# Layer-norm statistics of two tiles by one VectorE instruction, with reordered logits, stores and waits, in a fused attention and expert kernel

## The chip, the cores and the metric

The kernel runs on one core of a Trainium2 chip. The metric is the device time of one execution in microseconds; the time of the kernel before is the median of three runs. The engines are PE (TensorE), VectorE (DVE), ScalarE (ACT), GpSimd (POOL) and the DMA queues, the first of which SyncE (SP) issues.

## What is computed

The reference, cut to what matters. `x` has 32 sequences of 256 tokens of 128 numbers; there are 8 experts with a hidden width of 512.

```python
h = _layernorm(x) * (1 + ca) + sa
x = x + ga * _L0_attn_ref(h, ...)
h = _layernorm(x) * (1 + cb) + sb
x = x + gb * _L0_ffn_ref(h, ...)

# attention, per sequence, cumulative sums along the tokens
K = exp(linear(x, Wk1, bk1)); K_cum = cumsum(K) + 1e-06
S = cumsum(K * V) / K_cum;    Q = sigmoid(linear(x, Wq1, bq1))
O_ar = S * Q
E = V[1:] - O_ar[:-1]
K2 = sigmoid(0.02 * linear(shifted x, Wk2, bk2) / sqrt(D))
S2 = cumsum(K2 * E);          O_ma = S2 * Q2
out = linear(O_ar + O_ma, Wproj, bproj)

# experts: each token goes to the expert of its largest logit
assign = argmax(x @ centroids.T)
xn = (x - mean(x)) * rsqrt(var(x) + 1e-05) * ln_g[e] + ln_b[e]
y = x + relu(xn @ W1[e] + b1[e]) @ W2[e] + b2[e]
```

So there are three layer norms: of x, of the sum after the attention (called z here), and of the rows of each expert tile.

## The kernel before

**Chunk stage.** The 64 tiles of 128 tokens are worked on in 16 chunks of four tiles (two sequences). A loop over c, written out for each engine by hand, runs several chunks at once: x statistics are made for chunk c + 5 on VectorE (`x_stats`, `x_means`), normalised on GpSimd (`normalise_x`, L493) for chunk c + 3, transposed on PE (L793) and scaled on ScalarE (`turned_x`, L947) for chunk c + 2; keys, k2 and q products follow (L735, L742, L745), VectorE makes the cumulative sums (`k_sum` L1188, `kv_sum` L1200, `error_sum` L1234, which makes S2), and PE adds up x, the shift, Oar and Mp products in one bank (L757, L759, L766, L783). ScalarE copies the sum to the row buffer (`sum_of`, L912). For chunk c - 1 VectorE makes the z statistics (`z_stats`, `z_means`), GpSimd normalises z two steps behind (L501), PE transposes it (`turn_z`, L691), ScalarE scales it (`turned_z`, L920), and for chunk c - 3 PE makes the logits (L714) and turns the result back (`turn_back`, L691 on h2T), which ScalarE writes to the rows (`rows_of`, L926). Every second step VectorE routes eight tiles (`route`, `place`) and PE makes rank products (`ranks`, L680 and L685). GpSimd scatters rows of 385 numbers to the expert regions in DRAM (`scatter`, L538) and multiplies the projection weights with the gates in c = 0 to 5 (`gate_weights`, L509).

**Statistics.** A `bn_stats` of 128 numbers writes six values: count, mean and count times variance of the even elements, then of the odd ones. `bn_aggr` joins them to mean and variance in `mv`. ScalarE turns the mean to its negative (`minus_means`, L933) and makes exp(-0.5 ln(var + eps)) (L1014, L1025); the first four chunks get their negative mean on VectorE and their power on GpSimd (`first_rstd`).

**Plan.** After chunk 9 VectorE makes a first plan of expert tiles (`plan_first`), some of it in step c = 14. ScalarE reads expert numbers of the plan with `expert_of` (L296).

**Expert stage.** 36 tiles: 25 of 256 rows of one expert, then 11 of two blocks of 128 rows. For tile j: load (SP, L442 or L447), statistics (`tile_stats`, L1462, `tile_means`, L1469) three tiles ahead, normalisation (L1475), transposes (L830), ScalarE's `norm_of_expert` (L1064), first layer (L817, or L821 for blocks), relu (L1044, L1051, for blocks the last part on VectorE, L1484), second layer (L845), VectorE's bias, residual and gate (L1501, L1674, L1692, L1709), and GpSimd's indirect stores of tile j - 2 (`store`, L613). `take_ids` (L605) makes the row numbers of a store from the loaded rows, three tiles ahead.

**What sets the order.** Every engine has its own queue and works it off in the order written. A wait for a semaphore at the head of a queue holds up all that is behind it. Nothing is scheduled by a program. `keep_going(n)` is n transposes of an identity into an unused bank.

## Time and profile before

| | us |
|---|---|
| median of three runs | 334.05 |
| lowest and highest | 332.75, 334.86 |
| the profiled execution | 336.69 |
| its span, first to last instruction | 335.0 |

| engine | busy us | share of the span | instructions |
|---|---|---|---|
| PE matmuls | 297.9 | 89% | 1889 |
| VectorE | 268.0 | 80% | 926 |
| ScalarE | 248.6 | 74% | 556 |
| GpSimd | 237.4 | 71% | 370 |

The mean granted clock of PE is 0.964: the profile shows stretches at 1.2 GHz instead of 2.4 GHz between 10 and 50 us, one near 165 us, and the end. The chunk stage takes the first 168 us or so, a stage in which both overlap follows to about 194 us, and the expert stage runs to 320 us. The rest is the last stores. Busy time of an engine says little by itself: where an engine waits, what it waited for must be read from the chain of waits (what released what) and the timeline (instructions in order of time).

### The profile page before, as it was taken

To read this page: it belongs to the slowest core of one execution; us is meant where nothing else is said; L and a number is where in the kernel's file an instruction comes from. 1 tells how busy PE (TensorE), PEld (TensorE's weight loads), DVE (VectorE), ACT (ScalarE), POOL (GpSimd) and SP (SyncE) were. 2 spreads that over 40 slices of the span, in tenths; PEclk is the share of its full clock that TensorE was granted. 3 is DMA by queue.
4 is the path that set the end of the run, shared out by engine and by line. 5 is a ranking of instruction groups with operands and counts; after the bars stand their busy time and mean duration, and the time that the engine had idled before them with its cause. 6 is when DMAs were issued, how large, how long until landed. Compare 5 with 4: busy or idle time off the path is not lost.

```text
span 335.0 us, 8136 instructions
## 1 busy us (share of the span) xinstructions
PE 297.9 (89%) x1889; PEld 237.1 (71%) x1889; DVE 268.0 (80%) x926; ACT 248.6 (74%) x556; POOL 237.4 (71%) x370
## 2 busy tenths in 40 slices
PE   8797998898989989899898999999999999888930
PEld 7474555564656656465587899999999999888930
DVE  5798999999999999989886387898666665758850
ACT  2759788989899999999768666776677776766510
POOL 7984334787989888978646878778888855544770
PEclk9979779999999999999799999999999999999985
DMA  7343288424438786634396789877888777778300
GB/s 213 80 117 94 80 241 217 127 63 155 157 116 233 208 233 200 168 103 149 104 291 206 229 269 302 284 238 228 229 226 234 208 238 226 220 232 233 102 18 0
DMA packets 49429, 60.87 MB, mean 182 GB/s; under 512 B 5557, under 2 KB 38095, under 8 KB 49379
## 3 DMA queue, kind: packets, MB, share of 16 engines
q1 hardware_dynamic: 42806, 43.11, 47.0%
q0 software_dynamic: 6368, 16.82, 13.7%
q8 instruction: 17, 0.28, 0.3%
q10 hardware_dynamic: 208, 0.41, 0.3%
q14 instruction: 30, 0.25, 0.3%
HBM read 39.90 MB, written 20.87 MB: 181 GB/s over the span
## 4 chain that ended last, share of the span: by engine, by line
PE 53%; DVE 13%; issue 13%; ACT 11%; POOL 3%; SPq 2%; DMA 1%; POOLq 0%; ACTq 0%; DVEq 0%
PE bank L845 15%; PE bank L817 13%; PE bank L639 3%; PE bank L821 3%; PE bank L742 2%; POOL out_dram L613 2%; PE bank L745 2%; PE bank L783 2%; DVE shared L1234 2%; PE bank L735 2%; PE bank L691 2%; PE bank L830 2%; PE bank L766 2%; ACT shared L947 2%; PE bank L714 1%
## 5 line engine op out<-in xcount | busy, mean ns | idle before, releaser
L613 POOL DMA_INDIRECT out_dram<-shared,ids x71 | 72.1, 1015 | 34.2 <-DVE shared L1709 15.9
L538 POOL DMA_INDIRECT expert_rows<-rows,slots x64 | 65.5, 1023 | 15.8 <-issue 15.4
L845 PE MATMUL bank<-w_all,shared 128*128 x568 | 69.4, 275 | 0.4 <-issue 0.3
L845 PEld LDWEIGHTS bank<-w_all,shared 128*128 128x128 f32 x568 | 66.2, 192 | 0.9 <-issue 0.9
L1044 ACT ACTIVATE shared<-bank,par 128x256 f32<-128x256 f32 x100 | 40.9, 472 | 15.3 <-PE bank L817 15.3
L501 POOL TENSOR_SCALAR zz<-rows,negm,rstd 128x128 f32<-128x128 f32 x64 | 33.4, 532 | 24.8 <-ACT rstd L1025 17.3
L817 PE MATMUL bank<-shared,early 128*128 128x256 f32 x200 | 47.8, 382 | 0.3 <-ACT shared L1044 0.3
L817 PEld LDWEIGHTS bank<-shared,early 128*128 128x128 f32 x200 | 36.1, 190 | 4.5 <-issue 0.3
L493 POOL TENSOR_SCALAR xh<-x_in,negm,rstd 128x128 f32<-128x128 f32 x64 | 28.6, 458 | 9.0 <-DVE shared L1207 8.6
L1501 DVE TENSOR_TENSOR shared<-bank,b_bc 128x256 f32<-128x256 f32 (+1 forms) x42 | 14.7, 366 | 23.6 <-PE bank L845 22.9
L1064 ACT ACTIVATE shared<-bank,par 128x256 f32<-128x256 f32 (+1 forms) x46 | 22.7, 515 | 6.4 <-PE bank L830 4.0
L821 PE MATMUL bank<-shared,rows 128*128 128x128 f32 x168 | 21.9, 278 | 2.9 <-DVE shared L1484 2.9
L1051 ACT ACTIVATE shared<-bank,par 128x128 f32<-128x128 f32 x64 | 18.8, 370 | 7.2 <-PE bank L821 7.1
L783 PEld LDWEIGHTS bank<-wg,Mp 128*128 128x128 f32 x128 | 17.5, 199 | 7.7 <-issue 7.7
L821 PEld LDWEIGHTS bank<-shared,rows 128*128 128x128 f32 x168 | 20.1, 192 | 3.9 <-DVE shared L1484 3.9
L959 ACT ACT_TABLE_LOAD x16 | 20.5, 1283 | 0.3
L954 ACT ACT_TABLE_LOAD x16 | 20.5, 1283 | 0.3
L979 ACT ACTIVATE blnv<-bmv,epsv 128x2 f32<-128x2 f32 (+1 forms) x36 | 10.5, 293 | 13.4 <-issue 7.1
L766 PE MATMUL bank<-wg,shared 128*128 128x128 f32 x128 | 19.9, 302 | 0.0
L757 PE MATMUL bank<-x_in,ident 128*128 128x512 f32 x32 | 17.0, 614 | 3.2 <-ACT rows L912 3.2
L1188 DVE TENSOR_TENSOR_SCAN shared<-seq_mask,bank 128x512 f32<-128x512 f32 x16 | 19.4, 1212 | 0.5 <-ACT bank L964 0.5
L920 ACT ACTIVATE h2T<-bank,mod 128x256 f32<-128x256 f32 x32 | 16.3, 559 | 4.3 <-PE bank L691 4.3
(216 smaller groups left out, 699.6 us busy)
## 6 DMA issues: line engine op xcount, KB each, us to landing
early<-in_L_ffn_W_dram SPq DMA_DIRECT2D x25, 256.0 KB
x_in<-expert_rows SPq DMA_DIRECT2D x15, 385.0 KB, 4.2
rows<-in_L_ffn_W_dram SPq DMA_DIRECT2D x21, 256.0 KB
x_in<-in_L_attn_x_dram SPq DMA_DIRECT2D x16, 256.0 KB, 3.2
rows<-gates_rows SPq DMA_DIRECT2D x32, 128.0 KB, 5.2
full<-expert_rows SPq DMA_DIRECT2D x10, 385.0 KB
expert_rows<-pad_rows SPq DMA_DIRECT2D x9, 385.0 KB, 8.4
full<-expert_rows SPq DMA_DIRECT2D x11, 192.5 KB
```

The source lines that it names most:

```text
L493: pool.tensor_scalar(xh[:, a % 2, t, :], x_in[:, a % XR, t, :], negm[:, a, 0, t:t + 1], rstd[:, a, 0, t:t + 1], ALU.add, ALU.mult).then_in ...
L501: pool.tensor_scalar(zz[:, y % 2, t, :], rows[:, y % RR, t, W:W + D], negm[:, y + 6, 1, t:t + 1], rstd[:, y + 6, 1, t:t + 1], ALU.add, ALU ...
L538: pool.indirect_dma_start(rows_dram, bass.IndirectOffsetOnAxis(ap=slots[:, c * CN + t:c * CN + t + 1], axis=0), rows[:, c % RR, t, :], Non ...
L613: pool.indirect_dma_start(out_rows, bass.IndirectOffsetOnAxis(ap=ids[:, u % IR, t:t + 1], axis=0), u_sb[:, k, t, :], None, bounds_check=T - 1,
L766: pe.matmul(ps_proj[:, t * P:(t + 1) * P], Oar[:, c % 2, s, l:l + P], wg[:, CS * c + s, :], start=False, stop=False)
L783: mm = pe.matmul(ps_proj[:, t * P:(t + 1) * P], Mp[:, c % 2, s, l:l + P], wg[:, CS * c + s, :], start=False, stop=(t == CN - 1))
L817: mm = pe.matmul(hidden_at(j, f), w1_of(j, 0)[:, f * P:(f + 1) * P], zT[:, j % 2, :], start=True, stop=True)
L821: mm = pe.matmul(hidden_at(j, f)[:, t * P:(t + 1) * P], w1_of(j, t)[:, f * P:(f + 1) * P], zT[:, j % 2, t * P:(t + 1) * P], start=True, st ...
L845: mm = pe.matmul(out_at(o, t), hid[:, k, f, t * P:(t + 1) * P], of_expert(w2_all, e, f * D, (f + 1) * D), start=(f == 0), stop=(f == FC - 1))
L954: act.activation(lnK[:, q % 2, :, :], Kc[:, :, :], ACT.Ln, scale=LN_SCALE, bias=epsk[:, :]).then_inc(s_ln, 1)
L1044: r = act.activation(hid[:, j % 2, f, :], hidden_at(j, f), ACT.Relu, bias=par[:, 2 + f, bass.ds(e, 1)])
L1064: z = act.activation(zT[:, n % 2, h], ps_t[:, h], ACT.Identity, bias=par[:, 1, bass.ds(e, 1)], scale=par[:, 0, bass.ds(e, 1)])
```

## The change

Statistics:

- One `bn_stats` reads two tiles with their elements alternating, so that its even elements are those of one tile and its odd elements those of the other. Its six values then are count, mean and 128 times the variance of each. `bn_aggr`, `xbn`, `zbn`, `mv` and `negm` are gone; the values stay in `bn`, whose room is kept for every step. ScalarE's logarithm takes a scale of 1/128.
- GpSimd subtracts the mean itself; the negations on ScalarE and VectorE are gone.
- In the expert stage a tile with a single block reads it twice. The statistics wait for what `bn_aggr` waited for.
- At c = 14 the z statistics stand behind `error_sum`.

Order and waits:

- PE makes the logits and turns them back ahead of the Oar products.
- PE runs eight more identity transposes at c = 14, ahead of the k2 and q products.
- `gate_weights` of c = 2 to 5 waits for the `error` of one step later.
- ScalarE reads the first two expert numbers at c = 15 ahead of `rows_of`, and `rstd_of(14)` stands ahead of `sum_of(15)`.
- GpSimd takes the ids of tile j behind the stores of iteration j, not those of tile j + 3 ahead of them.

The diff, cut to its core:

```diff
-        mv = sb("mv", [P, STEPS, 2, CN, 2])
+        bn = sb("bn", [P, STEPS, 2, CN, 3])
...
-                    pool.tensor_scalar(zz[:, y % 2, t, :], rows[:, y % RR, t, W:W + D], negm[:, y + 6, 1, t:t + 1],
-                                       rstd[:, y + 6, 1, t:t + 1], ALU.add, ALU.mult).then_inc(s_zz, 1)
+                    pool.tensor_scalar(zz[:, y % 2, t, :], rows[:, y % RR, t, W:W + D], bn[:, y + 6, 1, t, 1:2],
+                                       rstd[:, y + 6, 1, t:t + 1], ALU.subtract, ALU.mult).then_inc(s_zz, 1)
...
-                    pool.wait_ge(s_E, c + 1)
+                    pool.wait_ge(s_E, c + 1 if c < 2 else c + 2)
...
-            for j in range(-3, NJ + 2):
-                if in_b(j + 3):
-                    take_ids(j + 3)
+            for j in range(NJ + 2):
...
+                if in_b(j):
+
+                    take_ids(j)
...
+                if in_a(z):
+                    logits(z)
+                    turn_back(z)
+                if in_a(c):
                     pe.wait_ge(s_Oar, c + 1)
...
-                if in_a(z):
-                    logits(z)
-                    turn_back(z)
...
+                if c == NC - 2:
+
+                    keep_going(8, ps_t)
...
-                    act.activation(lnv[:, i, kinds, :], mv[:, i, kinds, :, 1], ACT.Ln, bias=epsv[:, :]
+                    act.activation(lnv[:, i, kinds, :], bn[:, i, kinds, :, 2], ACT.Ln, scale=1.0 / D, bias=epsv[:, :]
                                    ).then_inc(s_lnv, 1)
-                    minus_means(i, kinds)
...
+                if c == NC - 1:
+
+                    act.wait_ge(s_planned, 1)
+                    of_first = [expert_of(act, n) for n in range(2)]
                 if in_a(z):
                     rows_of(z)
...
             experts = [norm_of_expert(0)]
+            rstd_of(NC - 2)
             sum_of(NC - 1)
-            rstd_of(NC - 2)
             experts.append(norm_of_expert(1))
...
+            def stats_of_two(into, rows_of_two):
+
+                return dve.bn_stats(into.rearrange("p t k -> p (t k)"), rows_of_two.rearrange("p t d -> p d t"))
...
-                dve.bn_stats(zbn[:, t, :], rows[:, o % RR, t, W:W + D]).then_inc(s_bnz, 1)
...
+                stats_of_two(bn[:, o + 6, 1, 2 * h:2 * h + 2, :], rows[:, o % RR, 2 * h:2 * h + 2, W:W + D]
+                             ).then_inc(s_bnz, 1)
...
-                for t in parts(n):
-                    dve.bn_aggr(bmv[:, n % 4, t, :], bbn[:, n % 4, t, :]).then_inc(b_aggr, 1)
+                two = full(n)[:, :, 0:D] if len(parts(n)) == FS else full(n)[:, 0:1, 0:D].to_broadcast([P, FS, D])
+                stats_of_two(bbn[:, n % 4, :, :], two).then_inc(b_bn, 1)
...
-                if in_a(o):
+                if in_a(o) and not first:
                     z_stats(o, 0)
-                    z_stats(o, 1)
...
+                if first:
+                    z_stats(o, 0)
                 if in_a(o):
-                    z_stats(o, 2)
-                    z_stats(o, 3)
+                    z_stats(o, 1)
...
-                if in_a(a) and c >= 0:
+                if in_a(a):
                     x_stats(a, 0)
                     x_stats(a, 1)
-                if in_a(a) and c >= 0:
-                    x_stats(a, 2)
-                    x_stats(a, 3)
-                    for t in range(CN):
-                        x_means(a, t)
```

The first place is VectorE in a chunk step without routing, from the product with k2 to the ratio of the next step. `rows` holds z and `x_in` holds x. Before:

```order
L1228 SCALAR_TENSOR_TENSOR bank<-bank,shared 128x2x255
L1142 BN_STATS zbn<-rows 128x6 x2
L1234 SCALAR_TENSOR_TENSOR shared<-seq_mask,bank 128x512
L1142 BN_STATS zbn<-rows 128x6 x2
L1240 SCALAR_TENSOR_TENSOR Mp<-bank,shared 128x2x256
L1147 BN_AGGR mv<-zbn 128x2 x4
L1131 BN_STATS xbn<-x_in 128x6 x4
L1136 BN_AGGR mv<-xbn 128x2 x4
L1207 TENSOR_TENSOR shared<-shared 128x512
```

The same piece of VectorE's order in the changed kernel, where line numbers are some ten lower:

```order
L1221 SCALAR_TENSOR_TENSOR bank<-bank,shared 128x2x255
L1129 BN_STATS bn<-rows 128x6
L1227 SCALAR_TENSOR_TENSOR shared<-seq_mask,bank 128x512
L1129 BN_STATS bn<-rows 128x6
L1233 SCALAR_TENSOR_TENSOR Mp<-bank,shared 128x2x256
L1129 BN_STATS bn<-x_in 128x6 x2
L1200 TENSOR_TENSOR shared<-shared 128x512
```

Eight statistics instructions and eight aggregations of a step have become four statistics instructions; each stands where its pair stood.

The second place is PE at c = 14, from the z transposes to the Mp products; `centT` marks the logits, the transposes of h2T are `turn_back`, and the products of `wg` and `shared` are those with Oar. Before:

```order
L691 MATMUL bank<-ident,zz 128x128 x4
L757 MATMUL bank<-x_in,ident 128x512
L759 MATMUL bank<-shift_in,ones_bf 128x512
L766 MATMUL bank<-wg,shared 128x128 x4
L714 MATMUL bank<-centT,h2T 128x8 x4
L691 MATMUL bank<-ident,h2T 128x128 x4
L742 MATMUL bank<-shared,wT 128x512
L745 MATMUL bank<-shared,wT 128x512
L783 MATMUL bank<-wg,Mp 128x128 x4
```

The same piece of PE's order in the changed kernel:

```order
L688 MATMUL bank<-ident,zz 128x128 x4
L754 MATMUL bank<-x_in,ident 128x512
L756 MATMUL bank<-shift_in,ones_bf 128x512
L711 MATMUL bank<-centT,h2T 128x8 x4
L688 MATMUL bank<-ident,h2T 128x128 x4
L767 MATMUL bank<-wg,shared 128x128 x4
L636 MATMUL bank<-ident 128x128 x8
L739 MATMUL bank<-shared,wT 128x512
L742 MATMUL bank<-shared,wT 128x512
L784 MATMUL bank<-wg,Mp 128x128 x4
```

The Oar products have moved behind the logits and their way back, as in every step from c = 3 on, and eight identity transposes stand ahead of k2.

The third place is ScalarE between the stages, from the scaling of chunk 12 to the rows of chunk 13; L296 reads the plan. Before:

```order
L920 ACTIVATE h2T<-bank,mod 128x256 x2
L926 ACTIVATE rows<-bank 128x4x128
L979 ACTIVATE blnv<-bmv,epsv 128x2
L982 ACTIVATE brstd<-blnv 128x2
L920 ACTIVATE h2T<-bank,mod 128x256 x2
L979 ACTIVATE blnv<-bmv,epsv 128x2
L982 ACTIVATE brstd<-blnv 128x2
L296 TENSOR_LOAD plan
L296 ISA x2
L1064 ISA
L1064 ACTIVATE shared<-bank,par 128x256
L912 ACTIVATE rows<-bank 128x4x128
```

The same piece of ScalarE's order in the changed kernel:

```order
L921 ACTIVATE h2T<-bank,mod 128x256 x2
L293 TENSOR_LOAD plan
L293 ISA x2
L293 TENSOR_LOAD plan
L293 ISA x2
L927 ACTIVATE rows<-bank 128x4x128
L973 ACTIVATE blnv<-bbn,epsv 128x2
L977 ACTIVATE brstd<-blnv 128x2
L921 ACTIVATE h2T<-bank,mod 128x256 x2
L973 ACTIVATE blnv<-bbn,epsv 128x2
L977 ACTIVATE brstd<-blnv 128x2
L1065 ISA
```

Both reads of the plan have moved ahead of `rows_of(12)`, from the place just ahead of the first two `norm_of_expert`.

## Rows read from the trace of the kernel before

**Rows 1.** Windows by stage: from:to, length, busy PE, PEld, DVE, ACT, POOL, clock, DMA share, GB/s

```profile
52.00:149.00 97.00, 89.45 (x502) 58.32 (x503) 94.58 (x263) 91.03 (x162) 79.15 (x127) 1.00 0.58 166
...
194.20:277.50 83.30, 83.21 (x591) 77.29 (x590) 61.54 (x262) 58.51 (x157) 65.85 (x82) 1.00 0.82 243
```

**Rows 2.** Timeline of VectorE at c = 6: start us, length us, engine, line, what

```profile
84.55 0.47 DVE L1142 BATCH_NORM_STATS2 zbn<-rows 128x6 f32<-128x128 f32 x2
84.94 1.19 DVE L1234 TENSOR_TENSOR_SCAN shared<-seq_mask,bank 128x512 f32<-128x512 f32 x1
...
87.87 0.85 DVE L1131 BATCH_NORM_STATS2 xbn<-x_in 128x6 f32<-128x128 f32 x4
88.76 0.38 DVE L1136 BATCH_NORM_AGGREGATE mv<-xbn 128x2 f32<-128x6 f32 x4
89.05 0.77 DVE L1207 TENSOR_TENSOR shared<-shared 128x512 f32<-128x512 f32 x1
```

**Rows 3.** Chain of waits, 96 to 111 us: start us, length us, engine and line

```profile
99.31 0.45 PE bank L793 x4
...
100.95 0.63 PE bank L691 x4
...
106.02 0.86 PE bank L742 x2
...
108.70 0.44 PE bank L793 x4
```

**Rows 4.** Timeline of PE, z transposes of c = 3 and c = 13

```profile
51.98 0.63 PE L691 MATMUL bank<-ident,zz 128*128 128x128 f32 x4 [1.20 <-ACT shared L947]
...
148.95 0.63 PE L691 MATMUL bank<-ident,zz 128*128 128x128 f32 x4 [0.51 <-ACT shared L947]
```

**Rows 5.** Timeline of GpSimd, gate weights of c = 4 and three z normalisations

```profile
69.35 1.84 POOL L509 TENSOR_TENSOR wg<-wg,wT 128x256 f32<-128x256 f32 x2
...
77.65 2.17 POOL L501 TENSOR_SCALAR zz<-rows,negm,rstd 128x128 f32<-128x128 f32 x4 [1.46 <-ACT rstd L1025]
...
88.57 2.26 POOL L501 TENSOR_SCALAR zz<-rows,negm,rstd 128x128 f32<-128x128 f32 x4
...
97.72 2.29 POOL L501 TENSOR_SCALAR zz<-rows,negm,rstd 128x128 f32<-128x128 f32 x4
```

**Rows 6.** Groups by line and shape, VectorE: count, then busy us, mean ns, idle before

```profile
L1188 DVE TENSOR_TENSOR_SCAN shared<-seq_mask,bank 128x512 f32<-128x512 f32 x16 | 19.4, 1212 | 0.5 <-ACT bank L964 0.5
...
L1131 DVE BATCH_NORM_STATS2 xbn<-x_in 128x6 f32<-128x128 f32 x64 | 13.6, 274 | 0.6 <-DMA x_in<-in_L_attn_x_dram 0.6
...
L1194 DVE TENSOR_TENSOR bank<-bank,shared 128x512 f32<-128x512 f32 x16 | 11.0, 690 | 0.4 <-ACT shared L947 0.2
```

**Rows 7.** Line L1221: duration ns min/median/max; and its instruction of c = 5

```profile
L1221 DVE SCALAR_TENSOR_TENSOR shared<-shared x16: 678/682/1430, 19.7 to 168.8; 128x510 f32<-128x510 f32 x16
...
72.49 0.68 DVE L1221 SCALAR_TENSOR_TENSOR shared<-shared 128x510 f32<-128x510 f32 x1
```

**Rows 8.** Chain of waits, at the start

```profile
12.34 0.86 DVE xbn L1131 x4
```

**Rows 9.** Timeline of PE at c = 14, k2 and Mp products

```profile
163.24 1.31 PE L742 MATMUL bank<-shared,wT 128*128 128x512 f32 x2 [1.43 <-DVE shared L1234]
...
166.15 1.69 PE L783 MATMUL bank<-wg,Mp 128*128 128x128 f32 x8
```

**Rows 10.** Timeline of ScalarE between the stages, the first two `norm_of_expert`

```profile
176.24 0.56 ACT L1064 ACTIVATE shared<-bank,par 128x256 f32<-128x256 f32 x1 [0.86 <-PE bank L830]
...
178.31 0.56 ACT L1064 ACTIVATE shared<-bank,par 128x256 f32<-128x256 f32 x1 [0.50 <-issue]
```

**Rows 11.** Waits by engine and line, whole span: us in total, times, longest

```profile
PE bank L821 <- DVE shared L1484: 2.9, 4, 1.2
```

**Rows 12.** Timeline of GpSimd, first and last of the last seven stores

```profile
317.81 1.00 POOL L613 DMA_INDIRECT out_dram<-shared,ids  x1 [0.52 <-issue]
...
325.59 0.97 POOL L613 DMA_INDIRECT out_dram<-shared,ids  x1 [0.30 <-issue]
```

97 lines of the change are left out of this document (29 added, 68 removed).

## The prediction

> **What bounds the kernel now.** I read three views in this order: the windows by stage, the chain of waits, and the timeline of one engine at a time inside one chunk step.
>
> The windows [rows 1] give the stages. From 52 to 149 us VectorE is busy 94.6 of 97.0 us, while PE, ScalarE and GpSimd have 89.5, 91.0 and 79.2. From 194 to 277 us PE has 83.2 of 83.3 us and VectorE only 61.5: work taken from VectorE there is worth nothing. So the question is what the statistics cost inside a chunk step, and what the next limit is.
>
> The timeline of VectorE [rows 2] prices them by the distance between starts, since instructions overlap. Two statistics instructions of 128 elements take 84.94 - 84.55 = 0.39 us. Four x statistics and the wait for their last one take 88.76 - 87.87 = 0.89, the four aggregations and the wait for them 89.05 - 88.76 = 0.29. With two z pairs (0.78) and four z aggregations (0.28, nearly as for x) a step spends 2.24 us on statistics.
>
> The chain of waits [rows 3] shows the next limit. From the end of the x transposes at 99.31 + 0.45 = 99.76 to the z transposes at 100.95 PE waits 1.19 us for ScalarE (`turned_x`, L947). From there PE works without a pause to 108.70 + 0.44 = 109.14, that is 8.19 us. PE order and this one answer of ScalarE form a loop of 8.19 + 1.19 = 9.38 us that no edit here shortens: the moved logits are the same work inside it. Between the z transposes of c = 3 and of c = 13 lie 148.95 - 51.98 = 96.97 us, 9.70 a step [rows 4]. So at most 0.32 us a step can come back, although VectorE may lose three times that.
>
> GpSimd is as near. Its z normalisations start 9.15 us apart with scatters between them [rows 5], and the first of the two did not wait for `rstd`, so it had been running late.
>
> **The change part by part, in microseconds.**
>
> *Statistics.* Two tiles by one instruction of 256 elements, elements of both tiles alternating, and no aggregation. The trace has no such reading pattern. From below: 128 elements take 0.195 us between starts, and the plain 512-element rows have a mean of 690 ns against 274 ns for 128 here [rows 6], about 1.08 ns an element; 128 more give 0.195 + 0.14 = 0.33. From above: the scans, the slowest rate of VectorE in the trace, have 1212 ns for 512 elements [rows 6], 2.37 ns an element, so 256 give about 0.61 us. I take 0.33, since the row of the same operation is nearest. Then a step has 4 x 0.33 = 1.32 instead of 2.24, which is 0.92 less. VectorE falls to about 8.8 us a step, below the 9.38 loop.
> The Trainium skill speaks against this value: "Vector Engine (DVE) Microarchitecture Reference", section 5.2, says that a port is at full rate only for runs of two adjacent words, and gives 1.73 ns a column for one source that hops at every element. The same section excepts a one-source operation that alternates between two regions. No run here shows either yet. By the hopping price 256 elements would take some 0.50 us, 2.0 a step, and almost all of the gain in the loop would be gone; this is my second case below.
>
> *Loop, c = 3 to 12.* At most ten times 0.32 = 3.2. Rank products fill the 1.19 us after every second step and exceed it by up to 0.4 early on, so about 0.9 is not to be had. GpSimd takes more: `gate_weights` of c = 4 ran at 69.35 and now waits for the `error` of c = 5, L1221, which ended at 72.49 + 0.68 = 73.17 [rows 7], 3.8 us later; the only idle time behind it is the 1.46 before the z normalisation at 77.65 [rows 5], so GpSimd comes 2.3 us late and wins back about 0.2 a step. Against this, VectorE's L1221 no longer overlaps those weights: it has 682 ns at the median and 1430 at most [rows 7]. Taken: -1.5.
> The skill's "SBUF — State Buffer" says that a VectorE instruction with two SBUF inputs contends with a GpSimd one that reads SBUF; the row of L1221 agrees.
>
> *Start.* `x_all(3)` with its aggregations and negation lies on the chain; its four statistics alone have 0.86 [rows 8]. The next instruction needs the keys K, ready soon after. Taken: -0.4.
>
> *Steps 13 to 15.* At c = 14 the z statistics now stand behind `error_sum`, 0.39 off the way to S2, and one step of shorter statistics adds about as much; ScalarE's negation (0.2) goes. Taken: -1.0.
>
> *Keeping PE going.* At 163.24 PE has been idle 1.43 us for S2, and the three groups from there (k2, q, Mp) take until 166.15 + 1.69 = 167.84, 4.60 us [rows 9], at the granted half clock. At full clock the same stretch is 108.70 - 106.02 = 2.68 [rows 3]. Eight transposes of about 0.12 each (1.0) now fill the idle time, at no cost while the wait exceeds 1.0. If the clock stays at its upper level, that is worth 1.9. Taken: -1.9.
>
> *Between the stages.* ScalarE is the chain here. Two reads of the plan, 0.86 and 0.50 idle before the first two `norm_of_expert` [rows 10], move to a place where it waited for PE, three negations of 0.2 go, and `rstd_of(14)` no longer stands behind `sum_of(15)`. In the other direction the logits of chunk 12 now stand ahead of the Oar products, which must stand behind a wait for h2T of about 1.2; the z transposes of chunk 13 come some 0.5 later. 0.86 + 0.50 + 0.6 - 0.5, and 0.2 for the order. Taken: -1.7.
>
> *Expert stage.* To 277 us nothing: PE covers it. After it PE waits 2.9 us for the last relu on VectorE [rows 11], whose queue is held by a load; behind that load the statistics pair and aggregation shrink by about 0.2 in each of some seven tiles, half of it felt. Taken: -0.7.
>
> *Stores first.* GpSimd no longer waits for rows of tile j + 3 ahead of stores, but where it waits now it waits for VectorE's sums. At the end seven stores run without waiting from 317.81 to 325.59 [rows 12], and the last two id additions now lie among them. Taken: +0.2.
>
> Sum: -0.4 - 1.5 - 1.0 - 1.9 - 1.7 - 0.7 + 0.2 = -7.0. The profiled execution took 336.69 us (span 335.0), so the changed one would take 329.7. The median of the runs is 334.05, 2.64 less; perhaps some runs lack the half clock at 163 us, and then the 1.9 is not theirs to gain. With it 327.05, without it 328.95; I say 328.0.
>
> **The rivals.**
>
> *A, as summed (0.50):* 328.0. For it: the two loops are read off the chain.
>
> *B, the alternating read costs about 0.5 us (0.20).* VectorE stays the bound: loop -0.4, start -0.2, steps 13 to 15 -0.6, expert stage -0.2, the rest as before: -4.8, and 1.0 for the clock that not every run can gain: 330.2. For it: nothing in the trace reads like this. Against it: only one stream is read and little is written.
>
> *C, slower (0.07).* The same instruction is dearer still. Its place is the VectorE queue of the ten steps c = 1 to 10. At t us each the step grows by 4t - 2.24; the other gains are 5.5 less 1.0. It decides from t = (2.24 + 0.45) / 4 = 0.67 us on. At 0.8 the loop has +9.6: 334.05 + 9.6 - 4.5 = 339.1. Against it: even the scans' rate gives 0.61.
>
> *D, the waits come back elsewhere (0.23).* GpSimd's 2.3 us lateness reaches PE through the z transposes, which takes the 1.5 of the loop, and the half clock comes anyway, for instance in the new wait for h2T at c = 15, which takes the 1.9: 334.05 - 7.0 + 3.4 = 330.4. For it: a z normalisation of 2.26 us at 88.57 ended at 90.83, with no room before PE's next transposes at about 91.1.
>
> **How the numbers follow.** Within 1% of 334.05 is 330.7 to 337.4, about what can be told from no change. A lies below 330.7 but for a tail, B and D lie around it, a bit over half of each below: faster 0.70, within 1% 0.22, slower 0.08. The range reaches from A with nearly the whole loop gain and some more in the early half-clock steps (328.0 - 4.2 = 323.8) to B with 0.61 us an instruction, which adds some 2.4 to 330.2: 332.6.
>
> **What would show it.** Statistics on VectorE near 0.33 us between starts (0.5 is B, over 0.67 is C). z transposes 9.4 to 9.6 us apart from c = 3 to 13, waiting for ScalarE or for GpSimd but never for VectorE's sums. VectorE at about 0.93 busy there instead of 0.975. No half clock near 160 us, and k2, q and Mp in 2.7 us. The first `norm_of_expert` some 5 us earlier than 176.24. Unchanged tile periods to 277 us. I would be wrong if GpSimd shows no idle time at all in the loop, or if the granted clock falls in new places while PE waits for h2T.

## The result, and the profile after

| | us | ratio to before, 95% interval |
|---|---|---|
| before, median | 334.3 (332.75 to 334.86) | |
| after, median of four runs | 363.35 (360.09 to 367.95) | 1.079 (1.071 to 1.086) |
| after, the profiled execution | 360.09, span 358.0 | |

The four runs of after fall into two near 360 us and two at 366 and 368; the ratio compares the lower pair with before. By it the kernel is 26 us slower (29 by the medians), where 6 us faster was forecast. Group rows of the page of after (engine, operation, count, then busy us, mean ns of one, idle before):

```profile
L496 POOL TENSOR_SCALAR zz<-rows,bn,rstd 128x128 f32<-128x128 f32 x64 | 53.5, 843 | 8.6 <-DMA wg<-gates_rows 3.8
L489 POOL TENSOR_SCALAR xh<-x_in,bn,rstd 128x128 f32<-128x128 f32 x64 | 51.1, 808 | 4.3 <-DVE shared L1200 3.9
...
L688 PE MATMUL bank<-ident,zz 128*128 128x128 f32 x64 | 11.4, 305 | 25.7 <-POOL zz L496 25.5
L921 ACT ACTIVATE h2T<-bank,mod 128x256 f32<-128x256 f32 x32 | 16.3, 560 | 22.3 <-PE bank L688 22.3
```

GpSimd's two normalisations take 843 and 808 ns a tile. In before the same groups had 532 and 458 ns:

```profile
L501 POOL TENSOR_SCALAR zz<-rows,negm,rstd 128x128 f32<-128x128 f32 x64 | 33.4, 532 | 24.8 <-ACT rstd L1025 17.3
L493 POOL TENSOR_SCALAR xh<-x_in,negm,rstd 128x128 f32<-128x128 f32 x64 | 28.6, 458 | 9.0 <-DVE shared L1207 8.6
```

In after PE waits 25.5 us for the z tiles, and ScalarE 22.3 us for PE behind them. The window from 52 to 149 us of after answers to [rows 1] (columns as there):

```profile
52.00:149.00 97.00, 81.72 (x418) 54.60 (x418) 73.12 (x130) 74.37 (x124) 87.77 (x110) 0.89 0.54 156
```

VectorE fell from 94.6 to 73.1 us of busy time, since it does less and since everything else waits too; GpSimd rose from 79.2 to 87.8, and PE's granted clock fell from 1.00 to 0.89. The chain of waits of after gives the share of each engine; GpSimd has the largest:

```profile
POOL 35%; PE 31%; issue 12%; DMA 9%; SPq 4%; ACT 3%; DVE 2%; POOLq 1%; DVEq 0%; ACTq 0%
```

The timeline of GpSimd from 104 to 119 us of after shows a step:

```profile
104.40 3.32 POOL L496 TENSOR_SCALAR zz<-rows,bn,rstd 128x128 f32<-128x128 f32 x4
107.89 1.08 POOL L533 DMA_INDIRECT expert_rows<-rows,slots  x1 [0.17 <-issue]
109.27 0.96 POOL L533 DMA_INDIRECT expert_rows<-rows,slots  x1 [0.31 <-issue]
110.24 0.20 POOL L523 COPY rows<-token_no 128x4 int32<-128x4 int32 x1
110.41 3.12 POOL L489 TENSOR_SCALAR xh<-x_in,bn,rstd 128x128 f32<-128x128 f32 x4
113.70 1.09 POOL L533 DMA_INDIRECT expert_rows<-rows,slots  x1 [0.17 <-issue]
115.10 0.96 POOL L533 DMA_INDIRECT expert_rows<-rows,slots  x1 [0.30 <-DVE shared L1200]
116.10 3.13 POOL L496 TENSOR_SCALAR zz<-rows,bn,rstd 128x128 f32<-128x128 f32 x4
```

From one z normalisation to the next, 104.40 to 116.10, lie 11.70 us with no more than the gaps of 0.17 and 0.3 us that stand ahead of every scatter. GpSimd works without a pause. In before the same stretch of queue took 97.72 - 88.57 = 9.15 [rows 5]. Eight tiles at 0.35 us more are 2.8 us, and 9.15 + 2.8 = 11.95, 0.25 more than measured. The means hide why: a block of four z tiles took 2.26 us at 88.57 in before, but 1.75 in a run shown further down. The durations of L501 are (lowest, median, highest):

```profile
L501 POOL TENSOR_SCALAR zz<-rows,negm,rstd x64: 437/445/1010, 47.2 to 183.7; 128x128 f32<-128x128 f32 x64
```

One tile in most of the blocks takes 0.84 to 1.01 us for 0.44. In before all 13 tiles of x and z that took over 0.8 us ran while VectorE was at L1207 or L1221, two instructions that read and write `shared` alone; [rows 2] have such an L1207 at 89.05, inside the block at 88.57. Without it the queue of a step is about 9.15 - 0.5 = 8.65 us long, and 8.65 + 2.8 = 11.45. The z transposes of after are 11.71 and 11.51 us apart from c = 7 to c = 9.

The same sum holds for the ten steps from c = 3 to c = 13. What GpSimd waited for in before (51.98 to 148.95) and in after (50.56 to 168.06; us in all, times, longest):

```profile
POOL zz L501 <- ACT rstd L1025: 10.4, 5, 4.6
POOL expert_rows L538 <- issue: 7.2, 31, 0.3
```

```profile
POOL expert_rows L533 <- issue: 6.5, 28, 0.3
POOL wg L504 <- DVE shared L1214: 2.6, 3, 1.7
POOL zz L496 <- ACT rstd L1019: 0.9, 2, 0.6
POOL expert_rows L533 <- ACT rows L927: 0.3, 1, 0.3
POOL expert_rows L533 <- DVE shared L1200: 0.3, 1, 0.3
```

GpSimd is busy for 79.1 us there in before and for 106.5 in after, 27.4 more. Its waits for other engines shrink from 10.4 to 4.1 us and the gaps ahead of scatters ("issue") from 7.2 to 6.5. That leaves 27.4 - 6.3 - 0.7 = 20.4 us, and the ten steps are 20.5 us longer.

The statistics themselves came in as forecast. By line and shape, and in VectorE's timeline, in after:

```profile
L1129 DVE BATCH_NORM_STATS2 bn<-rows 128x6 f32<-128x256 f32 x32 | 13.2, 418 | 1.7 <-ACT rows L913 1.6
...
82.18 0.41 DVE L1129 BATCH_NORM_STATS2 bn<-rows 128x6 f32<-128x256 f32 x1
82.52 1.20 DVE L1227 TENSOR_TENSOR_SCAN shared<-seq_mask,bank 128x512 f32<-128x512 f32 x1
```

One instruction takes 418 ns on average and 82.52 - 82.18 = 0.34 us from start to start.

### The profile page after: what moved, and what is told of

It reads as the page before. It is cut to its first block, busy times and chain, and to the rows that moved or that the text cites. A ratio compares the mean times of both kernels' runs of the same rounds, so it can differ in the third digit from the quotient of the medians.

```text
span 358.0 us, 7786 instructions
## 1 busy us (share of the span) xinstructions
PE 302.9 (85%) x1897; PEld 240.4 (67%) x1897; DVE 250.6 (70%) x624; ACT 247.1 (69%) x538; POOL 280.8 (78%) x370
## 3 DMA queue, kind: packets, MB, share of 16 engines
HBM read 39.90 MB, written 20.87 MB: 170 GB/s over the span
## 4 chain that ended last, share of the span: by engine, by line
POOL 35%; PE 31%; issue 12%; DMA 9%; SPq 4%; ACT 3%; DVE 2%; POOLq 1%; DVEq 0%; ACTq 0%
PE bank L846 14%; POOL zz L496 13%; PE bank L818 10%; POOL expert_rows L533 10%; POOL xh L489 9%; DMA wg<-gates_rows 6%; PE bank L822 3%; PE bank L831 2%; POOL wg L504 1%; SPq L443 1%; DMA full<-expert_rows 1%; PE bank L688 1%; SPq L449 1%; SPq L450 1%; DMA x_in<-expert_rows 1%
## 5 line engine op out<-in xcount | busy, mean ns | idle before, releaser
L609 POOL DMA_INDIRECT out_dram<-shared,ids x71 | 73.6, 1036 | 34.2 <-DVE shared L1675 17.8
L533 POOL DMA_INDIRECT expert_rows<-rows,slots x64 | 66.9, 1045 | 15.9 <-issue 14.9
L496 POOL TENSOR_SCALAR zz<-rows,bn,rstd 128x128 f32<-128x128 f32 x64 | 53.5, 843 | 8.6 <-DMA wg<-gates_rows 3.8
L489 POOL TENSOR_SCALAR xh<-x_in,bn,rstd 128x128 f32<-128x128 f32 x64 | 51.1, 808 | 4.3 <-DVE shared L1200 3.9
L688 PE MATMUL bank<-ident,zz 128*128 128x128 f32 x64 | 11.4, 305 | 25.7 <-POOL zz L496 25.5
L921 ACT ACTIVATE h2T<-bank,mod 128x256 f32<-128x256 f32 x32 | 16.3, 560 | 22.3 <-PE bank L688 22.3
L688 PEld LDWEIGHTS bank<-ident,zz 128*128 128x128 f32 x64 | 7.3, 150 | 29.8 <-POOL zz L496 29.2
L754 PE MATMUL bank<-x_in,ident 128*128 128x512 f32 x32 | 20.8, 737 | 6.9 <-DMA shift_in<-shift_rows 3.6
L784 PEld LDWEIGHTS bank<-wg,Mp 128*128 128x128 f32 x128 | 16.7, 191 | 7.2 <-issue 7.2
L711 PEld LDWEIGHTS bank<-centT,h2T 128*128 128x128 f32 x128 | 17.9, 217 | 4.3 <-ACT h2T L921 2.5
L953 ACT ACT_TABLE_LOAD x16 | 20.5, 1283 | 0.3
```

Source lines behind the costliest of these rows:

```text
L489: pool.tensor_scalar(xh[:, a % 2, t, :], x_in[:, a % XR, t, :], bn[:, a, 0, t, 1:2], rstd[:, a, 0, t:t + 1], ALU.subtract, ALU.mult).then_ ...
L496: pool.tensor_scalar(zz[:, y % 2, t, :], rows[:, y % RR, t, W:W + D], bn[:, y + 6, 1, t, 1:2], rstd[:, y + 6, 1, t:t + 1], ALU.subtract, A ...
L533: pool.indirect_dma_start(rows_dram, bass.IndirectOffsetOnAxis(ap=slots[:, c * CN + t:c * CN + t + 1], axis=0), rows[:, c % RR, t, :], Non ...
L609: pool.indirect_dma_start(out_rows, bass.IndirectOffsetOnAxis(ap=ids[:, u % IR, t:t + 1], axis=0), u_sb[:, k, t, :], None, bounds_check=T - 1,
L688: mm = pe.transpose(dst[:, t * P:(t + 1) * P], src(t), ident[:, :])
L754: pe.matmul(ps_proj[:, :], ident[:, :], x_in[:, c % XR, :, :].rearrange("p t d -> p (t d)"), start=True, stop=False)
```

## The experiments

They ran on five chips; on which before and after ran is not on record. On two of them the kernel before took 334 us, on three 366 to 373 us. Every kernel is compared with the kernel before on its own chip, and times are compared across chips only as ratios. Line numbers shift by a few from kernel to kernel.

### Is it the subtract form?

**e1** undoes one part of the change. The negations go back to ScalarE (and VectorE for the first four chunks), and GpSimd adds:

```diff
-pool.tensor_scalar(xh[...], x_in[...], bn[:, a, 0, t, 1:2], rstd[...], ALU.subtract, ALU.mult)
+pool.tensor_scalar(xh[...], x_in[...], negm[:, a, 0, t:t + 1], rstd[...], ALU.add, ALU.mult)
```

> The kernel after with one part undone: GpSimd adds a negated mean again (add, mult), the negations stand on ScalarE (and on VectorE for the first four chunks) as in the kernel before. Everything else is that of after: one bn_stats for two tiles, logits first, the gate_weights wait, keep_going, the orders of stores and ScalarE. Theory S (the subtract form costs GpSimd about 0.35 us more per 128x128 tile, 808 to 843 ns for 458 to 532, and that alone made the kernel slow): the xh and zz lines fall back to 440 to 530 ns, POOL's busy time from 281 to about 237 us, and the time to the prediction's region plus the price of the negations (some 0.2 us of ScalarE per step, partly covered), 326 to 332 us. Theory W (the other edits, a new wait or the doubled logits order, bring the loss and the slow GpSimd only shares it): the xh and zz lines fall back, but the time stays above 345 us. Theory V (GpSimd is slowed by VectorE's statistics of two tiles, not by its own operation): the xh and zz lines stay near 790 ns and the time near 363 us.

Measured beside a before of 370.0 us: 0.985 (0.978 to 0.991), with xh at 445 ns, zz at 508 and POOL at 236.1 us busy. Theory S holds on its lines; W and V fall. As this chip was a slow one, the kernels e1 and after were put side by side on a chip with a before of 333.7 us:

> The kernel after, unchanged, beside e1 on one chip, so that the price of the subtract form is read without a change of chip. Theory A (as j1 and j2 bear out, 1.039 each beside an e1 of 0.98 to 0.985, both together about twice that): after 1.075 to 1.10 of before, 0.095 to 0.115 above e1. Theory B (the two overlap once GpSimd is the bound): after at 1.05 to 1.07.

> The kernel of e1 once more, beside the kernel after. It stood at 0.9845 and 0.9799 on chips with a before of 370 and 373 us. Expected 0.978 to 0.992 on any chip; on one with a before of 334 us this is 327 to 331 us, with 328.0 predicted for the whole change.

After: 364.4 us, 1.085 (1.077 to 1.094). e1: 332.4 us, 0.993 (0.989 to 0.998), a little above what was expected of it. The one difference between the two is the form of 128 GpSimd instructions, with the negations and waits that it needs; it costs 0.092 of the ratio, 31 us. The groups of e1 there:

```profile
L499 POOL TENSOR_SCALAR zz<-rows,negm,rstd 128x128 f32<-128x128 f32 x64 | 32.0, 510 | 16.2 <-ACT rstd L1030 11.7 <-ACT rstd L945 4.3
L491 POOL TENSOR_SCALAR xh<-x_in,negm,rstd 128x128 f32<-128x128 f32 x64 | 27.8, 446 | 5.4 <-DVE shared L1211 4.9
```

Against after GpSimd has 53.5 + 51.1 - 32.0 - 27.8 = 44.8 us less to do, 0.35 a tile.

**e2** is the other direction, the kernel before with this edit alone (`ALU.add` on `negm` becomes `ALU.subtract` on `mv`, the negations go):

> The kernel before with one part of the change alone: the negations are gone and GpSimd subtracts the mean that bn_aggr wrote, (subtract, mult) in place of (add, mult). Statistics stay as before, one tile at a time. Theory S (the subtract form costs 0.35 us more per tile): the xh and zz lines take about 790 ns, POOL gains 128 x 0.35 = 45 us of busy time, and the kernel takes 355 to 368 us, more than after if anything, since the statistics gain is missing. Theory P (it is where the mean is read from: a column inside the bn records, 12 bytes apart, in place of a column of its own): here the mean lies 8 bytes apart in mv, so that the lines would take something between 450 and 790 ns. Theory W (the loss is from the other edits): the lines stay at 440 to 530 ns and the time is 331 to 335 us, or a little under from the negations that are gone.

Measured: 1.069 (1.060 to 1.079), theory S, beside e1's 0.985 on the same chip. Its lines:

```profile
L499 POOL TENSOR_SCALAR zz<-rows,mv,rstd 128x128 f32<-128x128 f32 x64 | 53.4, 843 | 10.5 <-ACT rstd L1021 7.0
...
L492 POOL TENSOR_SCALAR xh<-x_in,mv,rstd 128x128 f32<-128x128 f32 x64 | 50.9, 802 | 5.2 <-DVE shared L1203 4.8
```

The same 843 and 802 ns with none of the other edits, and with the mean read from another place. This edit alone makes the kernel before 7% slower.

**e3** gives each of the four tiles an operation pair and a line of its own. It leaves out a right layer norm, so that only the durations are read; it ran once, in 380.0 us beside a before of 370.0:

```diff
+pool.tensor_scalar(o[:, 0, :], i[:, 0, :], m[:, 0, :], r[:, 0:1], ALU.add, ALU.mult)
+pool.tensor_scalar(o[:, 1, :], i[:, 1, :], m[:, 1, :], r[:, 1:2], ALU.subtract, ALU.mult)
+pool.tensor_scalar(o[:, 2, :], i[:, 2, :], m[:, 2, :], r[:, 2:3], ALU.mult, ALU.add)
+pool.tensor_scalar(o[:, 3, :], i[:, 3, :], m[:, 3, :], r[:, 3:4], ALU.mult, ALU.subtract)
...
```

> Each of GpSimd's four tiles of xh and of zz has an operation pair and a line of its own, in the kernel of e1. The computation is changed on purpose in the normalisation of x and z: xh tiles read the mean inside the bn record with the pairs (add, mult), (subtract, mult), (mult, add), (mult, subtract) in the order of the tiles; zz tiles read a column of negm with (add, mult), (subtract, mult), (mult, mult), and a subtract alone. Theory S (the operation decides): add, mult 440 to 450 ns at the second to fourth tile with either operand, every pair with a subtract about 790 ns with either operand. Theory P (the place of the operand decides): all four xh lines about 790 ns and all four zz lines about 445 ns. Under S it is open whether mult, mult and mult, add count as the fast ones; if only subtract is slow they take about 445 ns, if only add, mult is fast they take about 790 ns. [...]

By line and shape, in the order of busy time (L492 to L495 are the xh tiles as above; L503 to L506 the zz tiles: add mult, subtract mult, mult mult, subtract):

```profile
L504 POOL TENSOR_SCALAR zz<-rows,negm,rstd 128x128 f32<-128x128 f32 x16 | 12.8, 798 | 0.0
L493 POOL TENSOR_SCALAR xh<-x_in,bn,rstd 128x128 f32<-128x128 f32 x16 | 12.8, 797 | 0.0
L495 POOL TENSOR_SCALAR xh<-x_in,bn,rstd 128x128 f32<-128x128 f32 x16 | 12.7, 796 | 0.0
...
L506 POOL TENSOR_SCALAR zz<-rows,negm 128x128 f32<-128x128 f32 x16 | 10.1, 629 | 0.0
...
L505 POOL TENSOR_SCALAR zz<-rows,negm,rstd 128x128 f32<-128x128 f32 x16 | 7.9, 491 | 0.0
L494 POOL TENSOR_SCALAR xh<-x_in,bn,rstd 128x128 f32<-128x128 f32 x16 | 7.6, 478 | 0.0
L492 POOL TENSOR_SCALAR xh<-x_in,bn,rstd 128x128 f32<-128x128 f32 x16 | 7.1, 446 | 4.3 <-DVE shared L1217 3.9
```

Every pair with a subtract, in either place and with either operand, takes 796 to 798 ns on average; mult mult, mult add and add mult take 446 to 491. The averages of some lines hold a few tiles prolonged as above. Lowest, median and highest:

```profile
L494 POOL TENSOR_SCALAR xh<-x_in,bn,rstd x16: 439/443/983, 7.4 to 149.3; 128x128 f32<-128x128 f32 x16
L505 POOL TENSOR_SCALAR zz<-rows,negm,rstd x16: 442/444/977, 48.6 to 192.7; 128x128 f32<-128x128 f32 x16
L506 POOL TENSOR_SCALAR zz<-rows,negm x16: 592/597/1114, 49.1 to 193.2; 128x128 f32<-128x128 f32 x16
```

So the pairs without a subtract all take 443 to 451 ns at the median (L492 has 447, L503 451), and the subtract costs 0.35 us in either place. The operation decides (theory S), not where the mean lies. A subtract alone, with one scalar instead of two, still takes 597; no row has an add alone beside it.

### How 45 us on GpSimd become 30 us of the span

**j1** and **j2** are e1 with the subtract form back for xh alone and for zz alone:

> The kernel of e1 with the subtract form back for xh alone (64 tiles of 128x128, reading the mean from the record), zz adds the negated mean. 64 x 0.35 = 22 us more on GpSimd, 1.4 us per step. GpSimd was busy 7.9 of 9.7 us per step before, so 9.3 with one of the two, and 10.7 with both (after: 10.6 of 11.75). Theory B (GpSimd's sum decides: below a step of about 9.4 it is hidden): near e1, 0.985 to 1.01, and likewise for j2; with both it is above the bound, hence the jump to 1.079. Theory Z (its place decides: zz is what the transposes wait for): j1 near e1 (0.985 to 0.995), j2 near 1.03 to 1.05. Theory A (any 0.35 us counts alike): j1 and j2 each about halfway, 1.02 to 1.04.

> The kernel of e1 with the subtract form back for zz alone (64 tiles of 128x128), xh adds the negated mean. Theory B (GpSimd's sum decides): as j1, 0.985 to 1.01. Theory Z (zz is what the transposes wait for, 4 x 0.35 = 1.4 us later per step against about 0.5 us of slack): 1.03 to 1.05, well above j1. Theory A (any 0.35 us counts alike): 1.02 to 1.04, as j1.

Measured: 1.039 (1.031 to 1.047) and 1.039 (1.031 to 1.047), on a chip with a before of 366.0. e1 stood at 0.980 and 0.985 on other chips of this kind, so each brings half the loss or a little more, whichever of the two it is (theory A). That xh is normalised three chunks ahead of its use does not protect it: z stands behind it in the same queue. Theory B, which gave GpSimd slack up to a step of 9.4 us because its busy time is 7.9, falls. The busy time leaves out the gaps: with them the queue of a step has 8.65 us, and 8.65 + 4 x 0.35 = 10.05. The z transposes of j2 are 10.05 to 10.15 us apart from c = 8 to c = 11.

**g1** asks the same from another side: e1 with the negations made by GpSimd, two instructions of four columns a step.

```diff
+pool.tensor_scalar(negm[:, y + 6, 1, :], bn[:, y + 6, 1, :, 1], -1.0, None, ALU.mult)
 pool.wait_ge(s_rstd, y + 3)
...
-minus_means(i, kinds)
```

> The kernel of e1 (all edits of the change, GpSimd adds a negated mean) with the negation of four means made by GpSimd itself, ahead of its wait for rstd, in place of ScalarE's (190 ns per step there, 0.3 us of latency in its row). GpSimd gets two instructions of 128x4 elements per step, about 0.2 us each (its veps row: 194 ns), and has 17 of 97 us idle in the loop. Theory H (ScalarE's answer is on the loop's path, GpSimd's wait for rstd hides the negation): 1 to 3 us under e1, 0.976 to 0.983. Theory N (neither is on the path): 0.982 to 0.988. Theory M (GpSimd's own two instructions and their waits are on the path): above 0.988, with longer waits of the z transposes on zz.

Measured: one run at 336.0 us and five from 341.2 to 344.0, too scattered for an interval, beside a before of 333.9; the profiled run is one of the five, with a span of 341.0. All six lie above before, which is theory M. GpSimd's timeline there:

```profile
96.90 0.26 POOL L507 TENSOR_SCALAR negm<-bn 128x4 f32<-128x4 f32 x1
97.32 1.75 POOL L512 TENSOR_SCALAR zz<-rows,negm,rstd 128x128 f32<-128x128 f32 x4 [0.16 <-issue]
```

A negation for z holds the queue for 97.32 - 96.90 = 0.42 us, one for x for 0.35 (101.97 to 102.30 and alike). Where GpSimd has time to spare this costs nearly nothing: from c = 8 to c = 13 the z transposes take 149.93 - 101.86 = 48.07 us, for 47.57 in e1, with 3.9 us of negations in between. They fill waits of e1 for `rstd` (0.2 to 0.6 us a step), and four of the five z blocks take 1.75 us where e1's take 2.12 to 2.26, prolonged as above. Where it is late already, at the gate weights, the same work comes out whole and more: from c = 5 to c = 8 the profiled run has 35.02 us for 29.48. Another 6.7 us are lost from c = 13 to c = 18, where PE's granted clock from 149 to 180 us is 0.83, for 1.00 in e1. How much of that the clock brings, and how much the negations, is not told apart.

The starts of the z transposes, read from PE's timeline, say where in the run it goes (us; the last column is what follows c = 18; e4, h1, j1 and j2 ran on chips with a before of 366 to 373 us, whose longer waits fall into that column):

| kernel | c = 3 | c = 13 | c = 18 | end | 3 to 13 | 13 to 18 | rest |
|---|---|---|---|---|---|---|---|
| before [rows 4] | 51.98 | 148.95 | 184.27 | 335.0 | 96.97 | 35.32 | 150.7 |
| before, second profile (k1) | 48.61 | 146.32 | 180.58 | 332.1 | 97.71 | 34.26 | 151.5 |
| after | 50.56 | 168.06 | 206.49 | 358.0 | 117.50 | 38.43 | 151.5 |
| e1 | 48.03 | 144.10 | 177.30 | 327.9 | 96.07 | 33.20 | 150.6 |
| f1 | 47.75 | 143.79 | 179.12 | 331.4 | 96.04 | 35.33 | 152.3 |
| f2 | 48.05 | 143.15 | 175.73 | 326.2 | 95.10 | 32.58 | 150.5 |
| after, second profile (k2) | 53.12 | 174.06 | 210.97 | 362.0 | 120.94 | 36.91 | 151.0 |
| g1 | 47.92 | 149.93 | 189.83 | 341.0 | 102.01 | 39.90 | 151.2 |
| j1 | 53.42 | 161.86 | 196.65 | 377.2 | 108.44 | 34.79 | 180.6 |
| j2 | 46.89 | 150.58 | 192.06 | 373.5 | 103.69 | 41.48 | 181.4 |
| e4 | 47.94 | 143.04 | 176.90 | 364.7 | 95.10 | 33.86 | 187.8 |
| h1 | 46.48 | 141.64 | 179.62 | 362.8 | 95.16 | 37.98 | 183.2 |

From e1 to after: 2.5 us at the start, 21.4 in the ten steps, 5.2 in the last five, 0.9 behind. That is 30.1 of 30.1. These two ran on different chips; on e1's own chip the second profile of after (k2) has 5.1, 24.9, 3.7 and 0.4, 34.1 in all. In both, over seven tenths lie in the ten steps. Two of the rows behind the table, of after:

```profile
50.56 0.66 PE L688 MATMUL bank<-ident,zz 128*128 128x128 f32 x4 [1.64 <-POOL zz L496]
...
206.49 0.66 PE L688 MATMUL bank<-ident,zz 128*128 128x128 f32 x4 [1.52 <-POOL zz L496]
```

### What is the rest of the change worth?

**e4** is the kernel before with the statistics of two tiles alone (`stats_of_two`, no `bn_aggr`, the negated mean stays):

> The kernel before with the statistics of two tiles by one bn_stats and no bn_aggr; the negated mean stays, GpSimd adds it. Logits, gate_weights wait, keep_going, stores, ids and ScalarE's order are as before. The prediction put about 1 to 1.5 us on the middle loop and parts of the start and the expert stage to shorter statistics. Theory S1 (the statistics bring a third to a half of the forecast gain): 330 to 333 us, DVE busy time 20 us or more below the kernel before. Theory S2 (VectorE isn't on the path that sets the end): 333 to 335 us, DVE's busy time down all the same. Theory S3 (an instruction of 256 elements with alternating reads is in the way of others): above 336 us.

> The kernel of e4 again (statistics of two tiles alone, GpSimd adds a negated mean), beside three others on one chip, since the chip of e4 held the expert stage's transfers up by some 35 us and this could hide or give gains. Theory H (e4's gain of 1.9% was the loop's and stands on any chip): 0.980 to 0.985 here. Theory I (part of that gain was in the held-up stretch): f2, which adds the border edits, stood at 0.988 on a chip without the hole, so that this one would stand at 0.988 to 0.995.

Measured: 0.981 (0.975 to 0.987) on a chip with a before of 370 us, with VectorE at 252.0 us busy for 268.0. The second try, on a chip with a before of 372.6, had 364.7 us in the median (357.0 to 368.0), too scattered for an interval. The statistics alone bring about 2% on such a chip; on one with a before of 334 us they were not run alone. The trace of e4 says what they bring in the loop: 95.10 us from c = 3 to c = 13, for 96.97 and 97.71 in the two profiles of before. This part does not hang on the chip, since e1 takes 142.66 - 46.49 = 96.17 there and 96.07 on a chip with a before of 334. So 1.9 to 2.6 us are the loop's; whether part of the rest belongs to those chips stays open.

**k1** is the kernel before, for a second profile:

> The kernel before, unchanged, for a profile on the chip on which the experiments run. In the first four experiments the comparison runs of this kernel took 370 us where the runs shown ahead of the prediction took 334, and the kernels' own profiles show engines idle for some 30 us between 165 and 235 us, waiting for something outside the core. Theory C (that hole belongs to the chip, by slower transfers, and to no edit): if this run takes 368 to 376 us, its middle loop (52 to 149 us) is as in the profile of before (PE busy 89.5 of 97 us) and the hole stands between 165 and 235 us; if it takes 333 to 337 us, the hole isn't there. Theory D (the edits make the hole): this run has no hole, whatever its time.

It took 335.3 us on a chip without the hole (the 30 us or so of idle engines between 165 and 235 us), its comparison runs 333.9, and the hole isn't in its trace. What those other chips do longer was seen in the experiments' traces alone. Waits of e1 on the chip with a before of 370 us, between 165 and 235 us ("remote": the releaser is outside the core or in no queue that the trace names):

```profile
DVE shared L1498 <- remote: 24.9, 3, 12.1
ACT shared L1053 <- remote: 15.6, 4, 6.6
```

On the chips with 334 us no such line stands in e1's waits. So it goes with the chip; what is late there was not found.

**f1** and **f2** divide the other edits. f1 is e4 with those of the loop (logits ahead of the gate products, the later wait of `gate_weights`, the order of z statistics in the last chunks). f2 is e4 with those of the border (`keep_going(8)`, ScalarE's order and early reads of the plan, stores ahead of ids).

```diff
 # f2 against after, beside the negated mean
-pool.wait_ge(s_E, c + 1 if c < 2 else c + 2)
+pool.wait_ge(s_E, c + 1)
...
+pe.wait_ge(s_Oar, c + 1)
...
 if in_a(z):
     logits(z)
     turn_back(z)
-if in_a(c):
-    pe.wait_ge(s_Oar, c + 1)
...
-if in_a(o) and not first:
+if in_a(o):
     z_stats(o, 0)
...
```

> The kernel of e4 (statistics of two tiles, GpSimd adds a negated mean) with the edits of the middle loop alone: logits before the gate matmuls, the later gate_weights wait, z statistics behind route in the last chunks. keep_going, stores, ids and ScalarE's order are those of before. e4 stood at 0.981 of before, e1 (all edits but the subtract) at 0.985. Theory L (the logits order does what the prediction said, hides the chain from z to the table behind gate matmuls): 0.975 to 0.980, the waits of h2T's reader on zz below those of e4. Theory N (these edits are covered or cancel): 0.979 to 0.985, the same as e4 within what can be measured. Theory M (the wait for the gate exponents one chunk later makes GpSimd late and costs): above 0.985.

> The kernel of e4 with the edits at the stage's border alone: keep_going(8) in chunk NC-2, ScalarE reads the experts earlier and orders rstd_of and sum_of the other way, stores before ids. The middle loop is as in e4. The prediction put 1.9 us on keep_going and the clock, 1.7 on ScalarE's order, -0.2 on the stores (together 1.0% of 334). Theory K (they bring it): 0.970 to 0.976. Theory N (on this chip the border waits for transfers, or the terms were not there): 0.978 to 0.985, as e4. Theory M (the matmuls kept going push work back): above 0.985.

Measured on one chip with a before of 333.9: f1 0.995 (0.991 to 0.999), f2 0.988 (0.983 to 0.993). By their bounds both are theory M, but the bounds were set from e4's 0.981 on a chip with a before of 370, and say little here; what stands is that f2 is the faster of the two. The z transposes say what the loop edits do: they are 10.26 us apart once in e1, and 9.44 in f2 at the same place. First e1, then f2:

```profile
76.81 0.66 PE L691 MATMUL bank<-ident,zz 128*128 128x128 f32 x4 [1.42 <-POOL zz L499]
87.07 0.65 PE L691 MATMUL bank<-ident,zz 128*128 128x128 f32 x4 [0.73 <-POOL zz L499]
```

```profile
76.68 0.63 PE L691 MATMUL bank<-ident,zz 128*128 128x128 f32 x4 [1.20 <-ACT shared L950]
86.12 0.66 PE L691 MATMUL bank<-ident,zz 128*128 128x128 f32 x4
```

In e1 GpSimd waited 2.91 us for `error` ahead of its gate weights, and its z tiles were late for two steps. In all the loop edits cost 96.07 - 95.10 = 0.97 us from c = 3 to 13. f1 without the border edits has 35.33 us from 13 to 18 where e1 has 33.20; f1 also has the clock at 0.66 from 165 to 170 us.

**h1** is e1 with the old gate_weights wait, beside e1 on one chip:

> The kernel of e1 again (the kernel after with GpSimd adding a negated mean, nothing else undone). Theory H (edits add up): loop edits alone stood at 0.995 and border edits at 0.988, both with the statistics; with all of them 0.985 to 0.990, that is 329 to 331 us beside a before of 334. The prediction was 328.0 for 334.05 (0.982), with no price on GpSimd's side of the subtract. Theory I (the loop edits and the border edits are in each other's way): 0.992 or more.

> The kernel of e1 with GpSimd's gate_weights wait as before (one chunk earlier). Everything else is that of after with the negated mean. Theory G (the later wait is what the loop edits lose: in f1 the z transposes of the last chunks come at 174.8 and 179.1 us, in f2 without it at 171.2 and 175.7): 0.5 to 1% under e1. Theory N (it costs nothing, the loss is from the logits order): the same as e1 within 0.3%. The prediction gave the wait no price of its own and a rival with GpSimd's lateness 1.5 us.

Measured: e1 0.980 (0.975 to 0.985), h1 0.979 (0.974 to 0.985), before 372.6. h1 has the z transposes of this place 9.47 apart, so the late step is the wait's doing. With the wait as before and the logits still ahead of the Oar products, h1 takes 95.16 us from c = 3 to c = 13, as e4 and f2 do (95.10) with the old order of both: the reordered logits bring nothing there and cost nothing. In the time no gain is seen (theory N). The profiled run of h1 loses from c = 13 to c = 18 what it gained, with 37.98 us for 34.85 in e1's on the same chip and a clock of 0.56 from 155 to 160 us; whether that is the wait's doing or this one execution's is open.

**h2** is f2 without `keep_going(8)`:

> The kernel of f2 (statistics and border edits) without keep_going(8). The prediction put 1.9 us on keep_going, through the granted clock of the stretch from 149 to 200 us (0.97 before). Theory K (it holds the clock): 0.5% or more above f2's 0.988, with a granted clock of 0.95 to 0.98 in that stretch for f2's 1.00. Theory N (the clock is held by the rest, the gain is of ScalarE's order): 0.985 to 0.990 with the clock at 1.00.

> The kernel of f2 again (statistics of two tiles, border edits with keep_going, GpSimd adds a negated mean), beside h2 on the same chip. f2 stood at 0.988 on a chip with a before of 334 us, h2 (the same without keep_going) at 0.9685 on one with a before of 373. Theory K (keep_going helps): h2 comes out above f2 by 0.5% or more. Theory N (no difference): within 0.4%. Theory O (it costs, the matmuls it adds stand ahead of queries and the last logits): h2 under f2 by 0.5% or more.

> The kernel of h2 again (f2 without keep_going). Expected as at f2b: theory K above f2b by 0.5%, theory N within 0.4%, theory O under it by 0.5%. On a chip with a before of 334 us theory O would give 325 to 328 us, and a kernel under both of this study.

First 0.969 (0.962 to 0.975), with a before of 372.6, where f2 was not run; then, side by side with a before of 366.0, f2 0.986 (0.979 to 0.992) and h2 0.988 (0.983 to 0.994). That is theory N by its bounds, though intervals of 0.006 on either side do not exclude the 1.9 us (0.5%) that was forecast. The clock says more. From 149 to 180 us it is 1.00 in f2, and 1.00 in both profiles of h2 as well. And e1 had a stretch of half clock with the eight matmuls in place, where e4 without them had none (165 to 170 us, first e1, then e4, columns as in [rows 1]):

```profile
165.00:170.00 5.00, 5.00 (x33) 5.00 (x32) 2.02 (x7) 2.40 (x7) 1.78 (x3) 0.66 0.97 308
```

```profile
165.00:170.00 5.00, 4.54 (x39) 4.08 (x38) 2.40 (x8) 3.45 (x11) 2.06 (x3) 1.00 0.99 322
```

f1, without them, had it too. So the eight matmuls don't keep the half clock away, and a run can be free of it without them. e1 itself differs from run to run: its third profile has 1.00 there and 33.20 us from c = 13 to c = 18, the two with the half clock 34.84 and 34.85.

## Why the prediction was wrong, by its own steps

**The step that failed is in "Steps 13 to 15" and "Between the stages":** ScalarE's negations were counted as gone (0.2 each), and the other side of that edit, GpSimd's subtract in place of an add, had no term at all, as if both took the same time. No row of before showed a subtract of this shape on GpSimd, so it needed bounds from below and from above, as the statistics got them. It cost 0.35 us a tile, 2.8 a step, and 0.092 of the ratio, 31 us, against the 0.8 us that the negations were counted for.

**"GpSimd is as near" was right and not carried through.** [Rows 5] have two z normalisations 9.15 us apart, and the first of them waited for nothing. The prediction read this as GpSimd's step, 0.2 short of the 9.38 of PE's loop. (About 0.5 of the 9.15 is one prolonged tile; the queue itself has some 8.65 us, 0.7 short.) With a price for the subtract the prediction would have read 9.15 + 2.8 = 11.95 a step for 9.70, ten times 2.25 us, 22 in the loop; after has 117.50 - 96.97 = 20.5. The view of waits says the same without that reading: GpSimd waited for others 10.4 us in the ten steps, and 28 us were put on it. Rival D had the path, GpSimd's lateness reaching PE through the z transposes, at 1.5 us instead of 30, and rival C, the only slower one, put the dearer instruction on VectorE.

**Statistics: right.** 0.34 us between starts for a forecast of 0.33. Rival B falls with it. By the 1.73 ns a column that the Trainium skill's "Vector Engine (DVE) Microarchitecture Reference", section 5.2, gives for one source that hops at every element, the prediction's estimate was some 0.50. The measured 0.34 agrees instead with the exception that the section makes for a one-source read that alternates between two regions, 16 KiB apart there and 512 or 1540 bytes here.

**Loop -1.5: right in size where the subtract is away.** e1 has 96.07 us between c = 3 and 13, for 96.97 and 97.71 in the two profiles of before. Without the later gate wait (e4, f2, h1) it is 95.10 to 95.16, near the floor of 93.8: the statistics bring 1.9 or 2.6 us, and the wait takes 0.97 back, as the term for the late GpSimd had it, with one step of 10.26 us. VectorE's busy share is 88.54 of 97 us in e1, 0.91 for a forecast of 0.93.

**Start -0.4:** c = 3 comes 48.61 - 48.03 = 0.6 us earlier in e1 than in k1. In after it comes 1.9 later than in k1, and 4.5 in the second profile. The first three xh blocks, 3.1 to 3.2 us each for 1.7 to 2.0 in k1, lie on after's chain.

**Keeping PE going -1.9: wrong.** It was read off the one profiled execution, which had a half-clock stretch near 163 us. k1's window from 149 to 200 us has the clock at 1.00 without any help:

```profile
149.00:200.00 51.00, 46.72 (x327) 38.19 (x325) 39.83 (x167) 39.74 (x96) 37.48 (x58) 1.00 0.69 216
```

The prediction named this case ("some runs lack the half clock") and gave it half. What it had wrong is that the eight transposes decide: with them e1 had the half clock in two of three profiles; without them f1 had it, and k1, e4 and both of h2 had none. How often before has it can't be told from one profile with and one without.

**Steps 13 to 15 -1.0, and between the stages -1.7: about half there.** From 13 to 18, e1 has 33.20 us for 34.26 in k1. The two reads of the plan did move: ScalarE's first `norm_of_expert` start at 172.55 in k1 behind 1.35 us of idle time for the reads, and at 169.78 in e1 behind 0.47 for PE:

```profile
172.55 0.56 ACT L1064 ACTIVATE shared<-bank,par 128x256 f32<-128x256 f32 x1 [1.35 <-issue]
174.62 0.56 ACT L1064 ACTIVATE shared<-bank,par 128x256 f32<-128x256 f32 x1 [0.50 <-issue]
```

```profile
169.78 0.56 ACT L1076 ACTIVATE shared<-bank,par 128x256 f32<-128x256 f32 x1 [0.47 <-PE bank L834]
171.27 0.56 ACT L1076 ACTIVATE shared<-bank,par 128x256 f32<-128x256 f32 x1
```

That is 2.8 us earlier for a forecast of 5 from another profile, but 2.2 of it is there already at c = 13 (146.32 - 144.10). The border itself brings 0.55 us up to the first and 1.1 up to the second `norm_of_expert` (174.62 and 171.27). Which of the border edits brings it was not told apart, apart from `keep_going`.

**Expert stage -0.7, stores +0.2:** the rest behind c = 18 is 150.6 us in e1 for 151.5 and 150.7. No gain that can be told; the two terms were not tested singly.

**The sum.** Without the subtract and with the negations back (0.8 of the forecast's terms) 6.2 us were expected and 0.7% of 333.7, 2.3 us, were measured on a chip like that of the prediction. The missing 1.9 is `keep_going`'s. The remaining 2 us lie within what runs differ by: the profiled spans of k1 and e1 are 332.1 - 327.9 = 4.2 us apart (0.6 at the start, 1.6 in the loop, 1.1 from c = 13 to 18, 0.9 behind), near the 4.3 of the terms without `keep_going`, but k1's run stood 1.4 above the median of its kernel and e1's 2.8 below. Which of the small terms was too large stays open. On chips with a before of 370 us the same kernel stood at 0.985 and 0.980.

The prediction's last two signs of being wrong came nearly true. From 52 to 149 us GpSimd waited for other engines 3.8 us in all, for 10.4 in before. And the clock fell in new places (0.89 in that window), but while PE waited for z tiles, 15.1 us, and not for h2T. The second followed from the first: in e1, which differs by the subtract and its negations alone, the clock is at 1.00 there.

## A version that beats both

f2 has the statistics of two tiles, the negated mean, the old loop and the new border: 329.5 us beside a before of 333.9, 0.988 (0.983 to 0.993), and 0.986 (0.979 to 0.992) on another chip. After stands at 1.079 and 1.085. h2, the same without the eight transposes, can't be told from it (0.988 beside 0.986).

## What to carry to other kernels

When an edit swaps one operation for another on the same engine, as a subtract for an add here, price it as an unknown: find a row of that very operation, or give it bounds. Before putting anything on an engine, measure its slack by what it waits for other engines in that stretch, not by its busy share. GpSimd was 82% busy (79.2 of 97 us), but of the other 18 us 7.2 were gaps ahead of its own scatters and 10.4 were waits, 1.0 a step, where 2.8 a step were put on it. The distance between two starts of one line without waits gives the length of the queue, if no instruction in it is prolonged by another engine. A gain that rests on a stretch of low clock in one profiled execution needs a second profile before it is counted.

## What the runs showed of the hardware

- On GpSimd a `tensor_scalar` of 128x128 fp32 with two scalars takes 443 to 451 ns at the median as (add, mult), (mult, add) or (mult, mult), and 795 to 799 as any pair with a subtract; a single subtract takes 597 (e3). That is 0.35 us for 128 elements of each partition, 2.7 ns an element more. The Trainium skill's "GPSIMD Engine Reference", section 4.1, calls one-input elementwise work on GpSimd roughly line-rate. The nearest row of VectorE, a (subtract, mult) of the same size (L1475 in before), has 359 ns: the trace is near the page without a subtract and 2.2 times above VectorE with one.
- A GpSimd tile that overlapped one of VectorE's L1207 or L1221 took 842 to 1010 ns, for a median of 445, in before (13 of 15 overlaps; one more had 605 ns). No run was made to take the overlap away.
- An instruction of four columns on GpSimd whose result the next one waits for holds the queue for 0.42 us at a duration of 0.25 (g1), and costs the kernel that only where GpSimd has no waits left to fill.
- VectorE's `bn_stats` over 256 elements that alternate between two tiles, 512 bytes or more apart, takes 416 to 427 ns on average in after and 0.34 us from start to start, for 274 ns of 128 plain elements [rows 6], and its two half results are the two tiles' own mean and variance.
- The same kernel took 334 us on some chips and 366 to 373 on others, with the difference in one stretch of waits for something outside the core; ratios of two kernels moved by about 1% with it.
